# Four small moves in the order of a conditioned linear-attention kernel's first two turns and its tail

## The reference, cut to what matters

```
xn = _ln(x, ln_w, ln_b)
q = xn @ Wq + bq
k = xn @ Wk + bk + (1.0 - src_mask) * -1000000.0
q = softmax(q.reshape(b, t, h, dh), axis=-1)
k = softmax(k.reshape(b, t, h, dh), axis=1)
v = ((xn @ Wv + bv) * src_mask).reshape(b, t, h, dh)
att = einsum('bnhd,bnhl->bhdl', k, v)
y = einsum('bnhd,bhdl->bnhl', q, att).reshape(b, t, d)
scale, shift = split((silu(emb) @ W_emb + b_emb)[:, None, :], 2, axis=2)
hh = _ln(y, ln2_w, ln2_b) * (1.0 + scale) + shift
return x + silu(hh) @ W_out + b_out
```

## Time and profile before

| | |
|---|---|
| median of the runs before | 319.23 us (318.64 to 320.84, 3 runs) |
| profiled execution | 318.37 us |
| its span, first to last instruction | 316.6 us |
| mean granted TensorE clock | 0.977 |
| busy: TensorE, VectorE, ScalarE, GpSimd | 94%, 86%, 74%, 77% |
| DMA | 38.69 MB, mean 122 GB/s |

### The profile page before, as it was taken

The page is one execution under the profiler, slowest core; times in us unless marked ns, Lnnn a source line. Parts: engine busy times, 40 slices in busy tenths (PEclk is TensorE's granted clock), DMA queues, the critical chain, the costliest instruction groups (busy, mean ns, idle before and its releaser), DMA issues.

```text
span 316.6 us, 14367 instructions
## 1 busy us (share of the span) xinstructions
PE 296.5 (94%) x5542; PEld 253.8 (80%) x5542; DVE 272.4 (86%) x639; ACT 234.7 (74%) x588; POOL 242.3 (77%) x247
## 2 busy tenths in 40 slices
PE   7997978899999999999999999999998799997964
PEld 6586757788979888889888888989897688987864
DVE  3997889699989999999999999999996697976793
ACT  1555789487978988888979897989888388984350
POOL 2164869839898989999999999898989539784450
PEclk9999999799999999999999999999999799999889
DMA  6952734206363452718090807263424310100013
GB/s 206 332 182 56 225 123 140 99 3 196 108 178 127 113 185 82 217 50 249 5 293 1 262 37 216 82 173 126 144 89 113 126 66 8 66 4 3 4 66 133
DMA packets 28434, 38.69 MB, mean 122 GB/s; under 512 B 2417, under 2 KB 20465, under 8 KB 28402
## 3 DMA queue, kind: packets, MB, share of 16 engines
q1 hardware_dynamic: 27984, 37.94, 38.1%
q10 hardware_dynamic: 418, 0.30, 0.3%
HBM read 29.80 MB, written 8.45 MB: 121 GB/s over the span
## 4 chain that ended last, share of the span: by engine, by line
PE 81%; DVE 8%; issue 3%; POOL 3%; ACT 2%; POOLq 1%; DVEq 0%; ACTq 0%
PE bk L1059 28%; PE bv L1059 26%; PE by L1059 15%; PE by L1136 5%; PE bv L1127 4%; PE by L1115 3%; DVE xt_lo L871 2%; DVE ystat L934 1%; DVE q_s L846 1%; POOL xr L437 1%; DVE y_s L919 1%; ACT xt_hi L564 1%; ACT xhat L585 1%; DVE qmax L838 1%; PE bk L1127 1%
## 5 line engine op out<-in xcount | busy, mean ns | idle before, releaser
L616 ACT ACTIVATE k_t<-k_t,kmax 128x64 f32<-128x64 f32 x240 | 60.5, 337 | 9.2 <-DVE kmax L864 9.1
L281 POOL TENSOR_TENSOR z_s<-z_s,mod_shift 128x512 f32<-128x512 f32 x30 | 30.8, 1049 | 14.8 <-DVE z_s L878 14.8
L457 POOL TENSOR_TENSOR x_all<-x_all,bo_all 128x1024 f32 (+1 forms) x16 | 39.1, 2444 | 0.2
L417 POOL TENSOR_TENSOR h_lo<-h_s,h_hi 128x512 fp32r<-128x512 f32 x30 | 38.4, 1300 | 0.0
L428 POOL TENSOR_TENSOR xt_raw<-xt_raw,rows 128x512 f32<-128x512 f32 x28 | 36.1, 1291 | 2.2
L426 POOL TENSOR_TENSOR xt_raw<-xt_raw,rows 128x512 f32<-128x512 f32 x28 | 36.3, 1297 | 0.3 <-DMA rows<-rows_dram 0.3
L555 ACT ACTIVATE v_s<-bk,small 128x256 f32<-128x256 f32 x32 | 15.2, 476 | 24.5 <-PE bk L1059 23.2
L1059 PE MATMUL bv<-w_o_hi,h_hi 128*128 128x256 f32 x120 | 32.2, 289 | 0.0
L1059 PE MATMUL bv<-w_o_lo,h_hi 128*128 128x256 f32 x120 | 31.9, 287 | 0.0
L570 ACT ACTIVATE y_s<-y_s,yr 128x256 f32<-128x256 f32 x56 | 29.1, 591 | 3.3 <-POOL yr L449 3.2
L1059 PE MATMUL bk<-xt_hi,w_k_hi 128*128 128x512 f32 x64 | 26.7, 417 | 3.8 <-DVE q_s L846 3.5
(11 more groups left out here) (141 smaller groups left out, 864.5 us busy)
## 6 DMA issues: line engine op xcount, KB each, us to landing
x_all<-in_x SPq DMA_DIRECT2D x15, 512.0 KB, 6.4
out<-x_all SPq DMA_DIRECT2D x15, 512.0 KB, 3.4
xt_raw<-in_x_t SPq DMA_DIRECT2D x14, 512.0 KB, 5.1
rows<-rows_dram SPq DMA_DIRECT2D x14, 512.0 KB, 6.0
off<-in_mask_rows SPq DMA_DIRECT2D x16, 256.0 KB, 6.4
rows_dram<-xr_rows SPq DMA_DIRECT2D x56, 1.0 KB
x_all<-in_x SPq DMA_DIRECT2D x2, 256.0 KB, 3.4
z_s<-in_w_emb SPq DMA_DIRECT2D x1, 512.0 KB, 6.6
```

The source lines that it names most:

```text
L281: return eng.tensor_tensor(z, z, mod_shift[:, c, span(g, GB)].unsqueeze(2).broadcast_to([P, GB, SEQ]), ALU.add)
L417: nc.gpsimd.tensor_tensor(h_lo[:, c, :], h_s[:, c, :], h_hi[:, c, :].bitcast(fp32), ALU.subtract).then_inc(hlo_d, 1)
L457: nc.gpsimd.tensor_tensor(xg, xg, bo_all[:, :].unsqueeze(1).broadcast_to([P, T, D]), ALU.add).then_inc(xb_d, 1)
L616: last = nc.scalar.activation(kk, kk, ACT.Exp, scale=-1.0, bias=kmax[:, c, n:n + 1])
```

## The change

It moves four things. In turn 0, VectorE's x_rows(2) goes from its place ahead of q's second half to behind x_low(1). In turn 1, VectorE's y_stats(0) goes behind q's second half. In the tail, ScalarE's second e_k copy goes ahead of q's exp. And eight more dummy products stand on TensorE between the two half transposes of the last y.

```diff
             def tail():
                 exp_k_copied(L, 0)
+                exp_k_copied(L, 1)
                 q_exp(L, 1, 1)
-                exp_k_copied(L, 1)
                 q_copied(L)
                 z_tanh(M, th_of)
                 act.wait_ge(yr_d, 2 * L + 2)
...
                 q_shifted(i, par, 0)
                 if B:
                     y_scaled_all(i - 1)
-                    y_stats(i - 1, (0, 1, 2, 3))
+                    if not (isinstance(i, int) and i == 1):
+                        y_stats(i - 1, (0, 1, 2, 3))
                 if first(i):
                     weights_o()
-                    x_rows(2)
                 q_max(i, 1)
                 q_shifted(i, par, 1)
+                if isinstance(i, int) and i == 1:
+                    y_stats(0, (0, 1, 2, 3))
                 if first(i):
                     x_low(1, by[:, 2:4, :])
+                    x_rows(2)
                     modulation()
                     x_stats(3, 1)
...
                 for _ in range(12):
                     mm(bk_[0][:, 0:P], ident[:, :], ident[:, :], True, True)
                 half_y_transposed(0)
+                for _ in range(8):
+                    mm(bk_[0][:, 0:P], ident[:, :], ident[:, :], True, True)
                 half_y_transposed(1)
```

## The result

The changed kernel takes 319.39 us in the median of 12 runs (317.68 to 325.69), the kernel before, run in turns with it, 318.66 us (12 runs, 313.06 to 320.84). The ratio is 1.0113, 95% interval 1.006 to 1.0167: about 1% slower. The forecast was 318.9 us and no change. The time lies in the range, the sign does not hold: no speed-up of the tail paid for the fill.

What follows compares the result with a forecast made beforehand. TensorE was taken as the bound, so only its waits count. Fill +4.4, tail copies -2.6 and dummies -1.7 sum to +0.1 us, giving 318.5 from the profiled execution or 319.3 from the median; 318.9 was taken, range 315.8 to 322.0.

Steps and rivals of the forecast that it cites:

- What bounds the kernel: TensorE, 81% of the chain; time counts only where it waits, in fill and tail; turns 3 to 15 pass shifts on.
- Part 1: Turn 0, group 2's rows later: q_s gains 0.3 to 0.8 us, the transpose comes 2.7 us later.
- all move by 2.7 us: Turn 0, DMA queue behind the transpose: stores, rows load and group 4's x load, landing at 37.45, all 2.7 us later.
- the first rival: Fill: x load hidden after all; fill costs 1.1 to 2.1, tail gives 4.3: 315.2 to 316.9 us; chance 0.16.
- Part 2: Turn 1, y statistics behind q's second half: they end 3.4 us later; turn 2's q transposes come 3.4 us later.
- the collision's 0.9 us: Turn 1: x_low on VectorE holds up GpSimd's pow, adding 0.4 to 0.9 us, taken as 0.9.
- The low stretch at 47: Fill, TensorE gaps between 39.9 and 49.8: a lower clock afterwards costs 1.0 us, bounds 0 and 1.4.
- The fill as a whole: Start to turn 2: the fill edits and low clock together cost +4.4 us, bounds 1.1 and 5.0.
- the forecast case: Whole kernel: 317.4 to 320.2 us by whether the fill's low stretch comes, 318.9 taken; chance 0.45.
- Parts 3 and 4: Tail: e_k copies ahead of q's exp give 2.6 us; eight dummies remove a low clock stretch, up to 1.7 us.
- The second: Tail gives only the wait back, -1.6 and 0, clock falls anyway; fill +3.4 to +4.4: 320.2 to 321.5 us; chance 0.25.
- the third rival: Tail: dummies run at the lower clock, second half starts 1.8 us late; fill +4.4: 323.0 us; chance 0.11.

Runs made afterwards that it cites:

- e5: The kernel before, unedited, run as a control against the kernel before: ratio 0.9925, mean 317.5 ± 0.6 us.
- e11: Whole change, with the x load for group 4 issued ahead of group 2's row stores, against the kernel before: ratio 0.9995.
- e14: First repeat of e11 (whole change, x load for group 4 ahead of the row stores) against the kernel before: ratio 1.0113.
- e4: Only the move of y_stats(0) behind q's second half in turn 1, against the kernel before: ratio 0.9979, mean 318.2 ± 0.6 us.
- e10: Whole change, but x_low ahead of the y statistics in turn 1, against the kernel before: ratio 1.0186, mean 320.3 ± 0.45 us.
- e1: Only the two moves in the fill, tail as before, against the kernel before: ratio 1.0066, mean 320.4 ± 0.5 us.
- e18: The two fill moves with the x load for group 4 ahead of the row stores, old tail, against the kernel before: ratio 0.9922, mean 319.2 ± 0.9 us.
- e13: The kernel before with only the x load for group 4 issued ahead of the row stores, against the kernel before: ratio 0.9976, mean 314.5 ± 1.4 us.
- e16: The two tail moves with the x load for group 4 ahead of the row stores, against the kernel before: ratio 1.0096, mean 315.1 ± 0.5 us.
- e6: The whole change repeated, unedited, against the kernel before: ratio 1.0092.
- e15: The whole change run a third time, unedited, against the kernel before: ratio 1.0244.
- e17: Second repeat of e11 (whole change, x load for group 4 ahead of the row stores) against the kernel before: ratio 0.9878.

## Why the prediction was wrong, step by step

**What bounds the kernel.** Most steps of the fill held in the profile. Turns 5 to 12 pass every shift on unchanged, 16.9 us each, as the prediction assumed of turns 3 to 15; it did not look at the exit from the loop behind them, in turn 13. The stall there is 2.37 us before, 2.92 after, 2.11 in e5 and e11, and there is none in e14. One row each, of TensorE in the kernel before, the changed kernel and e11:

```profile
246.96 0.43 PE L1059 MATMUL by<-kv,q_t 32*64 32x33 f32 x22 [2.37 <-issue]
```

```profile
250.79 0.43 PE L1062 MATMUL by<-kv,q_t 32*64 32x33 f32 x22 [2.92 <-issue]
```

```profile
249.13 0.43 PE L1065 MATMUL by<-kv,q_t 32*64 32x33 f32 x22 [2.11 <-issue]
```

In the 19 profiles with the stall the instruction packet ahead of its end starts 11.0 to 11.5 us after turn 13's k transposes, in e14 the corresponding one 7.6 us after them; what makes a packet start when it does stays open. With the low stretch that mostly follows the stall (in all but e5, e11 and e14), the middle takes 183.0 to 189.0 us, and the same source gave 185.6 (e5) and 187.9.

**Part 1.** The gain ahead of q_s was forecast at 0.3 to 0.8 us and was 0.41 on the clock of the two profiles; the profile after was already 0.39 us late at q's first half of turn 0 (21.80 against 21.41), ahead of any edited order, so 0.8 is the fairer figure. The move of the transpose, 2.7 forecast, was 2.8. The x load was to land 2.7 later and landed 1.0 later; the step "all move by 2.7 us" failed, since the store to load path in front of it, taken as fixed, shrank by 1.2 us, and the landing by 0.6. That is the first rival by half, and VectorE got back a wait for v_s (1.23 us) that the prediction had filled.

**Part 2.** The y statistics end 3.0 us later (3.4 forecast). The pow grew from 1.02 to 1.92 us: the collision's 0.9 us was the forecast value, and e4 shows it by itself, e10 without it. The Trainium skill (SBUF — State Buffer, "SBUF: two separate sides") would have the two instructions exclude each other; x_low runs from 44.92 to 46.14, the pow ends at 47.01, 0.87 us behind it, and 1.02 us is what it takes alone. So it was held for 0.90 us, of the 1.05 us for which x_low still ran when it started, and the trace agrees to 0.15 us. The q transposes moved by 3.43 us against +3.4, partly by compensation: x brought less, and the y products started later because of TensorE's stall of 1.05 us (0.46 before), which the prediction had not seen. It looked at what the moved DMAs make wait on VectorE, and not at what the burst does to TensorE's instruction packets. The low stretch at 47 came, as forecast.

The fill as a whole: +4.4 forecast, bounds 1.1 and 5.0. The profiles' fill pieces differ by 2.9; the means give +2.5 ± 0.5 beside the old tail and +4.1 ± 0.5 beside the new one. That is inside the bounds, and between the first rival's 1.1 to 2.1 and the forecast case.

**Parts 3 and 4, the step that failed.** The prediction took -2.6 and -1.7 from the profile before. In that pair of profiles they are right: the tail piece is shorter by 3.9 us, attention starts without a wait, the second half's wait is filled. But of these 3.9 us, 2.7 were two low stretches (30.5 against 27.8) which that one execution had, and which the old tail has only in some: it has none in four of seven profiles. Without them the two moves are worth 27.8 - 26.6 = 1.2 us.

Taken over all executions, the tail moves measured -2.5 ± 0.4 us by themselves and -0.9 ± 0.6 beside the fill moves, where -4.3 stood in the sum; with 2.5 for the fill moves the latter gives the +1.6. So the term was mis-sized: the order was worth 1.2 us, and the rest was priced as if every execution had the profiled one's two stretches. The fill was forecast too dear as well (4.4 against 2.5). The two errors offset each other in part, so it is partly luck that the sum came within 0.5 us of the time.

Why the clock part shrinks further beside the fill moves stays open. By the clock records the tail moves save 1.9 ± 0.3 us of lost clock time alone and 0.6 ± 0.7 beside the fill moves. In all three profiles of kernels with the y statistics moved and the old tail (e1, e4, e18) the stretches are gone before the tail is touched. That the fill's shift moves them out is argued from these three, not shown: e13, which changes the place of one load only, had a tail without them as well, and the twelve executions of e1 lost no less clock time than the kernel before.

**The rivals.** The second, in which the tail gives only the wait back (-1.6 and 0) and the fill costs 3.4 to 4.4, has the right sign and the right kind of cause, with 320.2 to 321.5 against 319.4 measured; its mechanism, the clock falling in the new tail, did not occur: 11 of 11 profiles have the new tail at the full clock until the last 2 us or so. Its number does not fit either, by 0.8 us at the least. Worked out from the 318.4 that the third rival uses, the upper ends of the first and second would be 316.2 and 321.2, not 316.9 and 321.5; no conclusion hangs on that. The third, dummies at the lower clock, was seen in no profile.

Leaving aside e13, whose mean is too uncertain (314.5 ± 1.4), the lowest means are those of the tail moves alone, 315.4 ± 0.3, and the same with the early load of x, 315.1 ± 0.5: 2.5 to 2.8 us below the kernel before, though e16 is only 1.3 ± 0.8 below its own comparison. Neither needs the moves in the fill.

## What to carry to other kernels

Cut the span of every profile at an instruction that recurs, and compare the pieces: a gain worked out from one execution's slow stretches is worth only the share of executions that have them, and beside another edit that share can be different. Where the granted clock of every execution is on record, take the lost clock time off the spans before two kernels are compared: here the small costs of single moves showed only then. When a small step moves on an engine, read which loads stand behind its stores in the DMA queue, and put a load that nothing holds back ahead of them. Price an edit beside the other edits of the same change as well as alone: here two moves cost 0.0 and 0.3 us by themselves (± 0.6) and 2.5 ± 0.5 together, and the difference lay in the clock.

## What the runs showed of the hardware

A tiny operation of GpSimd (128x4) took 1.92 us beside a VectorE operation with two inputs in SBUF, and 1.02 without that neighbour: 1.92 at its place at the end of turn 1 in the nine profiles in which the y statistics end just ahead of x_low (after, e1, e4, e6, e11, e14, e15, e17, e18), 1.02 in the other eleven. TensorE's "issue" waits end 1.2 to 1.5 us after a 16 KB packet of the instruction queue has landed, in 96 of 96 cases; between 98 and 237 us of the kernel before, in the loop, no such packet comes. TensorE's "issue" stall at the exit from the loop is 0 to 2.92 us from profile to profile, and 2.92 and 2.09 in two profiles of the changed kernel. Low stretches of the clock ahead of the span's last one are 3.41 us long, or twice that, and two executions of one program have them at different places; the kernel before spread from 311.0 to 322.1 us, and its executions, grouped by lost clock time to the nearest multiple of 1.7 us, had means of 315.1, 317.0, 318.7 and 320.1 us for two, three, four and five of them. From the first of four 1 KB stores to the load of what they wrote it took 3.45 us from issue to issue at 25 us into the kernel before, and 2.23 at 28 us into the changed one.
